# A decoder layer on one core: self-attention on x in place, weight quantisation moved under cross-attention, the ends of the pipeline written out step by step

## The reference

```python
x = _layernorm(x + _L0_attn_ref(x))                # self-attention
x = _layernorm(x + _L0_xattn_ref(x, ctx, ctx, ...))
x = _layernorm(x + _L0_ffn_ref(x, w_gate, w_up, w_down))

# self-attention: for every position l, over the 32 sequences
scores = einsum('lnc,lmc->lnm', q, q) / 8          # q = x as (l, n, c)
msg = einsum('lnm,lmc->lnc', softmax(scores), q)   # attn = x + msg
# cross-attention: 8 heads of 64, linear
qh = softmax(Wq q, over the head's 64) / 8;  kh = softmax(Wk k, over l)
context = kh vh^T;  out = Wo (context^T qh) + bo;  out / |out| * g * 8
# feed-forward: 512 -> 1376 -> 512
mx_linear(silu(mx_linear(x, w_gate)) * mx_linear(x, w_up), w_down)
```

## Time and profile before

| | us |
|---|---|
| median of 3 runs | 826.04 |
| lowest, highest | 824.41, 826.75 |
| the profiled execution | 824.84 |
| its span | 823.0 |

### The profile page before, as it was taken

How to read it: one execution, slowest core, us unless ns; L and a number is a source line. 1 busy time by engine, 2 the same in 40 slices (tenths; PEclk the granted TensorE clock), 3 DMA queues, 4 the chain that set the end, 5 groups by cost and what they waited for, 6 DMA issues and landing times.

```text
span 823.0 us, 14703 instructions
## 1 busy us (share of the span) xinstructions
PE 667.7 (81%) x5264; PEld 371.6 (45%) x5264; DVE 641.4 (78%) x1152; ACT 528.5 (64%) x953; POOL 478.9 (58%) x538
## 2 busy tenths in 40 slices
PE   2112556464789999999999999999999885999994
PEld 1112546463334554455445544554455542555542
DVE  4466777777688788988898889888987447999995
ACT  1114987876377877787778777877787552455552
POOL 5123424232164787678767876787677643767663
PEclk9999975766599999999999999999999998999997
DMA  8997010111000000000000000000000000010111
GB/s 197 232 201 260 28 38 25 38 25 46 0 14 14 1 14 14 14 2 14 15 14 1 14 14 14 1 14 15 14 1 1 1 1 1 14 39 27 39 39 51
DMA packets 25836, 31.00 MB, mean 38 GB/s; under 512 B 4016, under 2 KB 16304, under 8 KB 25776
## 3 DMA queue, kind: packets, MB, share of 16 engines
q1 hardware_dynamic: 25776, 30.22, 14.2%
HBM read 26.02 MB, written 4.19 MB: 37 GB/s over the span
## 4 chain that ended last, share of the span: by engine, by line
PE 70%; DVE 8%; ACT 7%; issue 6%; DMA 5%; POOL 2%; SPq 1%; ACTq 0%; POOLq 0%; DVEq 0%
PE banks L1289 8%; PE banks L1250 8%; PE banks L1366 8%; PE banks L1279 8%; PE banks L1301 7%; PE banks L1260 7%; PE banks L1324 7%; PE banks L1215 6%; ACT big L883 5%; PE banks L1393 4%; DMA big<-in_L_ffn_w_down_dram 3%; DMA big<-in_L_ffn_w_up_dram 2%; PE banks L1339 2%; PE banks L1331 2%; DVE big L581 2%
## 5 line engine op out<-in xcount | busy, mean ns | idle before, releaser
L883 ACT ACTIVATE big<-banks 128x512 f32<-128x512 f32 (+3 forms) x352 | 199.1, 590 | 101.9 <-PE banks L1279 43.5
L494 POOL TENSOR_TENSOR big<-big 128x512 f32<-128x512 f32 x128 | 131.7, 1049 | 3.6 <-DVE big L717 3.6
L697 DVE TENSOR_REDUCE big<-banks 128x1 f32<-128x512 f32 x128 | 83.0, 682 | 50.0 <-PE banks L1250 48.9
L486 POOL TENSOR_TENSOR big<-big 128x512 f32<-128x512 f32 x64 | 81.2, 1269 | 56.1 <-ACT big L970 56.1
L1215 PE MATMUL banks<-big 128*128 128x128 f32 x256 | 55.9, 407 | 54.6 <-ACT big L883 54.6
L883 ACT ACTIVATE big<-big 32x256 f32<-32x256 f32 (+4 forms) x112 | 90.3, 834 | 1.1
L965 ACT ACTIVATE big<-banks,big 128x512 f32<-128x512 f32 x128 | 87.1, 682 | 3.9 <-DVE big L697 3.8
L703 DVE TENSOR_REDUCE big<-banks 128x16 f32<-128x1024 f32 x64 | 76.7, 1198 | 8.7 <-PE banks L1260 8.6
L970 ACT ACTIVATE big<-big 128x1024 f32<-128x1024 f32 x64 | 67.2, 1049 | 21.8 <-DVE big L708 21.8
L1279 PEld LDWEIGHTS banks<-ident,big 128*128 128x128 f32 x512 | 56.2, 143 | 53.4 <-issue 36.5
L522 POOL TENSOR_TENSOR big<-big 128x1376 f32<-128x1376 f32 x16 | 58.1, 3633 | 37.7 <-DVE big L585 37.7
(11 more groups left out here) (105 smaller groups left out, 1166.5 us busy)
## 6 DMA issues: line engine op xcount, KB each, us to landing
big<-in_x_dram SPq DMA_DIRECT2D x2, 2048.0 KB, 16.8
big<-in_x_dram SPq DMA_DIRECT2D x4, 1024.0 KB, 11.0
xt<-in_x_dram SPq DMA_DIRECT2D x1, 4096.0 KB, 13.9
big<-in_ctx_dram SPq DMA_DIRECT2D x16, 256.0 KB, 2.7
out_dram<-big SPq DMA_DIRECT2D x16, 256.0 KB, 2.1
big<-in_L_ffn_w_down_dram SPq DMA_DIRECT2D x4, 688.0 KB, 7.2
big<-in_L_ffn_w_gate_dram SPq DMA_DIRECT2D x10, 256.0 KB, 2.7
big<-in_L_ffn_w_up_dram SPq DMA_DIRECT2D x10, 256.0 KB, 2.7
```

The source lines that it names most:

```text
L486: pool.tensor_tensor(qfold[:, i % 2], e[:, :, :, 0:DH // 2], e[:, :, :, DH // 2:DH], ALU.add).then_inc(s.q_folded, 1)
L494: pool.tensor_tensor(e, e, r, ALU.mult).then_inc(s.p_ready, 1)
L697: dve.tensor_reduce(kneg[:, par, i:i + 1], bank[par], X, ALU.max, negate=True).then_inc(s.k_max_ready, 1)
L883: return act.activation(dst, src, ACT.Copy)
```

## The change

The loop bodies of self-attention go and every engine gets one written list of steps from start to end, with loops only for the steady tiles.

- **Loads.** SP sends the first down block and two gate/up blocks, then x in four pieces (`load_x`), the small weights, `xq` in two halves with its sequences ordered by parity, the other down blocks, ctx, three double blocks of gate and up. x is loaded twice, not three times. Later blocks are loaded one per tile, each ahead of that tile's ctx.
- **Scores in place.** ScalarE and VectorE copy the upper 64 partitions of `xt` to the lower 64 of `xsw` and the other way round. `scores` reads columns of x and its swapped copy with a stride of 512 elements over 64 partitions; there are 8 chunks of 16 positions, no padded blocks, no copies.
- **Messages** take strided columns of `xq` and 16 columns of `pT`, per quarter and parity, and `add_msg` adds on 128 partitions.
- **Weights.** Seven large blocks (4 down; 3 of 128 x 1024, gate and up together) are quantised around self-attention, with GpSimd doing the last multiplication. Sixteen blocks of 128 x 512 (`scale_item`, `shift_item`, `clip_item`, `dequant_item`, `transpose_item`, `copy_item`) go one per tile under cross-attention.
- **Cross-attention** of tiles 0 to 4 and of the last tiles, and all of the feed-forward's begin and end, are written step by step; `ET` shrinks from four slices to two.

```diff
-    CL = 8
+    CL = 16
...
-        AREA = 34736
+        AREA = 42400
...
+        def halves_of_x(rows):
+            return big[rows, 0:2 * T * L].rearrange("p (s t l) -> p s t l", s=2, t=T)
+        xt = cut(T * L).rearrange("p (t l) -> p t l", t=T)
+        xsw = cut(T * L).rearrange("p (t l) -> p t l", t=T)
...
+            load_aw(0)
+            for k in range(2):
+                load_item(k)
+            for piece in range(4):
+                load_x(piece)
...
+            load_xq(0)
+            load_xq(1)
+            for a in range(1, DN):
+                load_aw(a)
...
+            for t in range(2, T):
+                if t < ITEMS:
+                    load_item(t)
+                load_ctx(t)
...
+            def dequant_item(k):
+                n = item_rows(k)
+                dve.wait_ge(s.w_clipped, k + 1)
+                if k:
+                    dve.wait_ge(s.tr_ready, tr_no[k - 1, "w"] + 1)
+                dve.tensor_tensor(groups(wbf[0:n]), groups(w8[0:n]), spread(w_scale[0:n, k % 2], GX), ALU.mult
+                                  ).then_inc(s.w_quantized, 1)
+            def swap_down(piece):
+                dve.wait_ge(s.x_loaded[piece], 16)
+                dve.tensor_copy(xsw[C:P, 4 * piece:4 * piece + 4], xt[0:C, 4 * piece:4 * piece + 4]
+                                ).then_inc(s.swapped_down, 1)
...
+            def add_msg(c, h):
+                dve.wait_ge(s.msg_ready[h], c + 1)
+                for jj in range(2):
+                    m = bank[(2, 6)[h] + jj][:, 0:CL * T].rearrange("p (l t) -> p t l", l=CL)
+                    l0 = LG * (2 * h + jj) + CL * c
+                    r = xt[:, :, l0:l0 + CL]
+                    last = dve.scalar_tensor_tensor(out=r, in0=r, scalar=2.0, in1=m, op0=ALU.mult, op1=ALU.add)
+                last.then_inc(s.msg_added[h], 1)
...
+            for f in range(7, T - 5):
+                q_sum(f - 1, 2)
+                x1_stats(f + 1)
+                q_max(f, 0)
+                q_shift(f, 0)
+                clip_item(f)
+                k_max(f, 1, 0)
+                scale_x(f - 3)
+                k_max(f, 1, 1)
...
+                dequant_item(f)
...
+                k_max(f + 1, 0, 1)
+                scale_item(f + 1)
...
-                if t and par == 0:
-                    act.wait_ge(s.a_done, 4 * t - 3 + i)
-                copy(ET[:, par, i], bank[4 + n % 2]).then_inc(s.tr_copied, 1)
+                if (t or i >= 2) and par == 0:
+                    act.wait_ge(s.a_done, 4 * t - 1 + i)
+                copy(ET[:, par, i % 2], bank[4 + n % 2]).then_inc(s.tr_copied, 1)
...
+                else:
+                    act.wait_ge(s.tr_ready, aw_last + 1)
                 act.activation(Ysb, bank[7][:], ACT.Identity, bias=bo2[:, 0:1]).then_inc(s.y_biased, 1)
...
+            def scores(c):
+                if c == 0:
+                    pe.wait_ge(s.swapped_up, 4)
+                    pe.wait_ge(s.swapped_down, 4)
+                if c >= 2:
+                    pe.wait_ge(s.scores_shifted, c - 1)
                 for l in range(CL):
                     for j in range(4):
-                        v = xs[:, k, l, j]
-                        last = pe.matmul(bank[k][B * j:B * j + B, B * l:B * l + B], v, v, start=True, stop=True)
+                        h = j // 2
+                        v = halves_of_x(slice(C * h, C * h + C))[:, :, :, LG * j + CL * c + l]
+                        last = pe.matmul(bank[c % 2][B * j:B * j + B, B * l:B * l + B], v, v, start=True, stop=True)
                 last.then_inc(s.scores_ready, 1)
+            def messages(c, h):
+                pe.wait_ge(s.pT_ready, c + 1)
...
+                for l in range(CL):
+                    for jj in range(2):
+                        rows = slice(B * (2 * h + jj), B * (2 * h + jj) + B)
+                        for par in range(2):
+                            k = T * (par ^ h)
+                            last = pe.matmul(bank[(2, 6)[h] + jj][C * par:C * par + C, T * l:T * l + T],
+                                             xq[rows, :, CL * c + l], pT[rows, c, l, k:k + T], start=True, stop=True)
+                last.then_inc(s.msg_ready[h], 1)
...
+            scores(0)
+            scores(1)
+            project(0)
...
+            scores(5)
+            messages(0, 0)
+            project_wo()
+            project_b()
+            scores(6)
+            transpose_down(0, 0)
+            messages(1, 0)
...
+            messages(3, 0)
+            k_logits(0, 0)
...
+            messages(7, 0)
+            k_logits(0, 3)
+            messages(6, 1)
+            messages(7, 1)
+            transpose_k(0, 0, 0)
+            k_logits(1, 0)
...
+            for f in range(5, T - 4):
                 k_logits(f, 0)
...
                 k_logits(f, 2)
+                a_product(f - 1, 2)
+                sum_squares(f - 2)
+                transpose_item(f)
                 q_logits(f, 2)
...
+            a_product(T - 1, 3)
+            gate_up(0, 0)
+            spread_rn(T - 2)
+            transpose_p(T - 1, 0, 0)
...
+            down(T - 2, 1)
+            transpose_h(T - 1, 0)
+            transpose_h(T - 1, 1)
```

More of the change, by code:

```diff
@@ L642, in transpose_probs @@
+            def transpose_probs(c):
                 dve.wait_ge(s.probs_ready, c + 1)
[L643 to L658 removed]
@@ new lines, in _ @@
+            copy_xT(7)
+            silu(6, 2)
+            copy_h(4, 0)
+            silu(7, 0)
+            silu(7, 1)
+            copy_h(4, 1)
+            copy_xT(8)
+            silu(7, 2)
+            copy_h(5, 0)
+            silu(8, 0)
+            copy_h(5, 1)
+            silu(8, 1)
+            result(1)
+            copy_xT(9)
+            silu(8, 2)
+            copy_h(6, 0)
+            result(2)
+            copy_xT(T - 6)
+            result(3)
+            silu(9, 0)
+            copy_h(6, 1)
@@ L1136, in _ @@
+            result(9)
+            copy_h(T - 5, 1)
+            copy_h(T - 4, 0)
+            result(T - 6)
+            copy_h(T - 4, 1)
+            for u in range(16, T + 2):
+                if u - 1 in tiles:
+                    silu(u - 1, 2)
+                copy_h(u - 3, 0)
+                if u in tiles:
+                    silu(u, 0)
+                copy_h(u - 3, 1)
                 if u in tiles:
                     silu(u, 1)
+                result(u - 5)
                 if u + 1 in tiles:
@@ L1158, in _ @@
                 last.then_inc(s.proj_transposed, 1)
-            pe.wait_ge(s.proj_copied, 2)
-            for j in range(NJ):
-                last = pe.transpose(bank[4][:, C * j:C * j + C], won[:, P * j:P * j + P], ident[0:C, 0:C])
-            last.then_inc(s.wo_transposed, 1)
-            pe.wait_ge(s.wo_copied, 1)
-            for h in range(2):
-                rows = slice(C * h, C * h + C)
-                for j in range(NJ):
-                    for up in range(2):
-                        last = pe.matmul(bank[5 + h][C * up:C * up + C, C * j:C * j + C], wvn[rows, j], woT[rows, j],
-                                         start=True, stop=True)
@@ L1190, in _, with project_wo @@
-            for q in range(DN):
-                transpose_down(q, q % 2)
-            pe.wait_ge(s.w_copied, DN)
-            for h in range(EARLY):
-                transpose_gu(DN + h, h % 2, P)
-            def scores(c, k, first=False):
-                pe.wait_ge(s.xs_ready, c + 1)
-                if not first:
+            def project_wo():
+                pe.wait_ge(s.proj_copied, 2)
+                for j in range(NJ):
+                    last = pe.transpose(bank[4][:, C * j:C * j + C], won[:, P * j:P * j + P], ident[0:C, 0:C])
+                last.then_inc(s.wo_transposed, 1)
@@ new lines, in project_b, with transpose_down @@
+            def project_b():
+                pe.wait_ge(s.wo_copied, 1)
+                for h in range(2):
+                    rows = slice(C * h, C * h + C)
+                    for j in range(NJ):
+                        for up in range(2):
+                            last = pe.matmul(bank[5 + h][C * up:C * up + C, C * j:C * j + C], wvn[rows, j], woT[rows, j],
+                                             start=True, stop=True)
+                last.then_inc(s.b_ready, 1)
+            def transpose_down(a, r):
+                n = tr_no[a, f"d{r}"]
+                if r == 0:
+                    pe.wait_ge(s.aw_quantized, a + 1)
+                if n >= 2:
+                    pe.wait_ge(s.tr_copied, n - 1)
+                else:
+                    pe.wait_ge(s.b_copied, 2)
+                o = bank[4 + n % 2].bitcast(BF16)
+                f0, f1 = ((0, 8), (8, FT))[r]
+                for f in range(f0, f1):
+                    m = P if f < FT - 1 else FR
+                    last = pe.transpose(o[0:m, P * (f - f0):P * (f - f0) + P], awbf[:, a % 2, P * f:P * f + m], ident_bf[:])
+                last.then_inc(s.tr_ready, 1)
@@ L1221, in turn @@
-            def turn(i, ahead=True):
```

(14 more changed lines are left out.)

2650 lines of the change are left out of this document (2066 added, 584 removed), and 11 rows, old and new, of the table first_groups.

## The result

The changed kernel takes **816.51 us** (median of 4 runs, 811.65 to 817.55) against 825.47 for the kernel before beside it: ratio 0.988, 95% interval 0.984 to 0.992. The direction was right; the size was not. The forecast was 710 us, its range 668 to 765: the change brought 9 us where some 116 were expected.

A forecast was written before the change was run, and what follows sets the result against it. ScalarE was taken to bound self-attention, TensorE cross-attention and feed-forward. First stage to 105 us, plus 566 us of TensorE work, plus 37 us of losses, gave 708 us span, 710 us time; range 668 to 765.

The forecast's parts named there:

- x arrives and is swapped: Start of self-attention: scores start at 21 us; waiting for xq charged 2 us, bounds 0 and 8.
- Scores: Self-attention: 512 products in 1024 instructions on x in place, 15.1 us as before the change.
- Messages: Self-attention: 1024 small products in 2048 instructions take 52 us, bounds 25 and 246 us.
- What goes: Self-attention: copies and half-height additions go; VectorE's 52 us lies beside TensorE, ScalarE no longer near the bound.
- Cross-attention inside: First stage: TensorE also does projections, down blocks 0 and 1 and four key products of tile 0, about 11 us.
- The 6 us of bubbles: First stage: TensorE's loss while chunk 0 runs through its five engines, 6 us.
- Blocks under cross-attention: Steady cross-attention: sixteen moved weight blocks cost VectorE 2.9 us per tile; 0.8 us per tile charged, 13 us in all.
- rival B: Steady cross-attention: VectorE becomes the bound, period 29.6 instead of 28.4 us, total 736 us; chance 0.17.
- New waits: Cross-attention: waits for a large block's transposes and for ET's two slices, nothing beyond the 0.8 us per tile.
- Ends: Stage seams: losses of 4 us before the feed-forward, 8 us filling tile 0, 12 us in the last part.
- A (strides): Self-attention: strided small products hold the first stage, messages 44 us and scores 8 us more, some 762 us; chance 0.17.
- D, slower: Self-attention: message products do not overlap at all, 904 us at 120 ns an instruction; chance 0.03.

The follow-up runs named there:

- e1: Changed kernel with three quarters of the rearranged x (xq) left out, 1 MB loaded instead of 4 MB: 790.04 us (one run).
- e2: Changed kernel with the small score and message products reading neighbouring elements instead of strided ones, same number and size: 800.57 us (one run).
- e12: Changed kernel with both the edits of e1 and e2, a quarter of xq and neighbouring operands: 765.16 us (one run).
- e6: e4 with the conversion back of weight blocks 2 to 12 also moved from VectorE to GpSimd: 793.07 us, ratio 0.962.
- e10: e3 with TensorE's transposes of those 14 blocks left out as well: 782.04 us (one run), spacing 28.10 us.
- e3: Changed kernel without the quantising of 14 of the 16 weight blocks under cross-attention; transposes and copies stay: 784.59 us (one run).
- e4: Changed kernel with two small operations of each weight block (scale and inverse) moved from VectorE to GpSimd: 799.56 us, ratio 0.970.

## Why the prediction was wrong, step by step

The forecast had messages end at 105 us and the span at 708. Measured: 169.5 and 813.7. Of the 106 us too few, 64.5 are in the first stage and 41 behind it.

1. **x arrives and is swapped.** The start of the scores was right (20.4 for 21). The step failed in what it said of xq: it asked only when the data would be there, 31 to 42 us, and charged 2 us, bounds 0 and 8. The first half was in by 46 us and the second by 66, and the cost was not a wait for data (TensorE shows none) but 28.5 us in which it had no code (e1: 25.4 back). Rows 4 are of loads into 32 partitions, and the diff halved that number; the text took the row's time for a quarter of xq unchanged.
2. **Scores.** 15.1 us forecast, 31.6 measured. e2 gives 16.3 with neighbouring operands: the count and the row were right, and the stride, "no row has that", was given no bound of its own. It was worth a factor of 1.9. And 15.1 us from the first score to the last could not have come in any case: in an unbroken list code comes at 29 to 31 ns per product (e12). Before, chunks of 64 stood between waits (rows 3), in which code could arrive; that this is why they ran at 12 to 17 ns is argued, not tried.
3. **Messages.** 52 us forecast, 72.6 measured, 55.2 without strides. The sum was good to 6% without the stride, but partly by luck: it took 21.7 ns and a clock of about 0.67 to get 25, where these products take 14 ns at 1.00 and 25 at 0.50, and 0.50 is what was granted. The rest is again the stride. The Trainium skill, SBUF — State Buffer (Door 1: The DMA port swizzle, on cachelines), stated that rule, and the trace agrees: 31 for 16 ns and 35 for 27. The forecast quoted it and left it out of the sum. The Trainium skill, TensorEngine Tiling (Array Packing) (Performance Considerations), by which the forecast estimated 25 ns each, was called refuted by 12 ns. The runs bear the row out and not the page: 16 ns for the scores, and for the messages 14 ns at the high clock; their 27 is the low clock.
4. **What goes.** Right: VectorE is busy 59 us from 20 to 169.5 (forecast 52), ScalarE 20, neither near the bound.
5. **Cross-attention inside.** 11 us forecast, some 16 measured: each of tile 0's k products takes 2.08 us, not the 1.06 of rows 2, because the granted clock is 0.50, the level of 1.2 GHz, from 100 to 169.5 us, though TensorE is busy for 68.53 of 69.50. The 6 us of bubbles were 2.
6. **Blocks under cross-attention. The step that decided the second half.** It gave VectorE 2.9 us per tile from rows 8 and charged 0.8 to the period; measured 4.45, and a plain period of 29.70 for the 28.4 forecast. The rows were means over places with and without GpSimd at work (the conversions of L607 took 0.69 to 1.42 us); in this tile three of the six instructions fall beside GpSimd's. TensorE's transposes were right, 0.25 for 0.23. That 28.4 is what e6 gives (28.35), where VectorE is out of the way, is luck: the 0.8 was charged for VectorE's lateness, which measured 1.35 (29.70 less e6's 28.35), and the 0.68 that e10 leaves on TensorE was not in the sum at all. That makes rival B: it was written as a period of 29.6 and cost 19 us; the plain tile has 29.70. The steady tiles average 30.2, 24 us more than forecast over the 13 spacings from 241.9 to 634.8; the longest of them also show a lower clock.
7. **New waits.** Nothing was charged, and none shows among the larger ones.
8. **Ends.** The last part was better than forecast: 148.2 us from the last G product for 154 (before's 161.4 less the 7.4 that the seam was to save). The filling was worse: counting 14 periods of 28.4 back from there, 708 - 154 - 398 = 156, tile 1's G product was to come 51 us after the messages; it came 72.4 after them, at 241.9. VectorE looks like the bound there too, with 67.39 busy of 72.5; e3 and e4, which relieve it, both bring tile 1's spacing from 39.2 to 37.0, but e6 does not.

```profile
169.50:242.00 72.50, 61.24 (x381) 29.41 (x383) 67.39 (x99) 49.53 (x96) 52.25 (x54) 0.97 0.09 28
```

The sum: 64.5 in the first stage, 24 in 13 steady tiles, 21 in the filling, 2 in the last spacing (30.7), less 6 at the end, is 105.

**The chances.** Rivals A (strides) and B (VectorE) had 0.17 each and were priced as if only one could come. Both came, with a third that was not on the list; they sit in different stages and simply add. A range built from the rivals one at a time ended at 765. D, slower, stayed away, and with it the sign was safe.

## What to carry to other kernels

When rivals sit in different stages, price their sum too: the range must hold the case in which two come together. When work is moved beside another engine's, take its durations from rows where that engine is active, not from a mean; on a row such as 0.17 against 1.20 us the whole margin of a tile can hang. And when a load is reshaped, ask how many partitions it fills at once and what else, code included, comes through the same DMA engines at that time.

## What the runs showed of the hardware that was not expected

- **Code comes through the DMA engines, one packet for 128 small products, and bounds them.** With empty DMA engines a packet takes 3.7 to 4.0 us from the last, so an unbroken list of small products runs at 29 to 31 ns each at best, though one takes 16. Behind loads that hold the engines at 100 GB/s the stops are 4.7 to 10.1 us; with a quarter of these loads 3.5 us in all. Why the slow loads hold a packet of code for so long was not tried further.
- **Two queues double the rate only if their partitions lie well and the queues really interleave**: 102, 166 to 182 and 187 GB/s in the stretches named above; from 20 to 38 us they took turns.
- **Under small products the clock stayed low.** TensorE was busy for 98% of 100 to 169.5 us and was granted 0.50 for all of it; the clock rose once the k products, transposes and q products of cross-attention took over, after 170 us. Without strides it is the same (0.50 over e12's 103.5 to 109.9). What in the small products does that was not isolated. It cost the strided ones nothing, but it would cost neighbouring operands 25 ns for 14.
- **A stop of TensorE seems to cost twice.** The tiles of 31 to 34 us show a granted clock of 0.90 to 0.95 where the plain one has 1.00; with VectorE's load gone (e3) or smaller (e6) the clock is 1.00 there too, and the long tiles mostly vanish. What lowers the clock was not tried by itself. The longest steady tile of the kernel after:

```profile
513.13:547.53 34.40, 31.20 (x193) 15.69 (x192) 30.44 (x50) 21.25 (x42) 23.00 (x30) 0.90 0.05 14
```

It has 193 products as every plain tile does, but 31.20 us of TensorE's time for them instead of 28.52.
